# A graph kernel's adjacency build: where TensorE transposes a group of blocks, and when the group is copied out

## The reference

```python
edge_index = jnp.stack([src, dst])
h = jnp.maximum(_layernorm(x), 0.0)
x = x + _L0_gnn_ref(h, edge_weight, src, dst, ...)       # weighted mean over neighbours, both ways, GRU
h = jnp.maximum(_layernorm(x), 0.0)
x = x + _L1_gnn_ref(h, src, dst, edge_weight, alpha)     # 3 hops: segment_sum(w * X[col], row)
h = jnp.maximum(_layernorm(x), 0.0)
x = x + _L2_gnn_ref(h, edge_index, ...)                  # 4 orders: segment_sum(x[row], col) / deg, and attention
h = jnp.maximum(_layernorm(x), 0.0)
x = x + _L3_gnn_ref(h, edge_index, edge_weight1, ...)    # a message per edge, summed by destination
```

## Time and profile before

| | |
|---|---|
| median of 3 runs | 4118.98 us (4118.73 to 4122.45) |
| the profiled execution | 4140.43 us |
| its span in the trace | 4138.6 us |
| busy in the span: PE / DVE / ACT / POOL | 86% / 35% / 31% / 21% |
| build stage, from the first tile to the start of the last window | 50 to 1107 us |
| tiles built; spans; groups copied | 1132; 250; 175 |

### The profile page before, as it was taken

How to read it: one execution, slowest core, us unless ns; L and a number is a source line. 1 busy time by engine, 2 the same in 40 slices (tenths; PEclk the granted TensorE clock), 3 DMA queues, 4 the chain that set the end, 5 groups by cost and what they waited for, 6 DMA issues and landing times. The chain is left out here.

```text
span 4138.6 us, 86265 instructions
## 1 busy us (share of the span) xinstructions
PE 3573.1 (86%) x24482; PEld 2462.8 (60%) x24483; DVE 1462.7 (35%) x4278; ACT 1265.7 (31%) x4012; POOL 873.6 (21%) x929
## 2 busy tenths in 40 slices
PE   5888889999989889968999999997878877877777
PEld 2345556777744444435999999984444545554455
DVE  6766667777602200024321111232222222222223
ACT  5566667788701200014322211232000000000001
POOL 2000000000010000000000000124666666665554
PEclk8999999999999999987999999997988889988889
DMA  2011222323494689851432222341222222222222
GB/s 60 1 46 62 72 67 92 107 94 123 137 233 116 146 197 240 195 139 32 130 107 77 77 77 75 90 114 46 66 64 62 62 62 62 65 63 58 56 59 58
DMA packets 120057, 381.81 MB, mean 92 GB/s; under 512 B 33166, under 2 KB 74620, under 8 KB 106026
## 3 DMA queue, kind: packets, MB, share of 16 engines
q1 hardware_dynamic: 90958, 324.81, 28.9%
q0 software_dynamic: 25664, 51.90, 5.2%
q10 hardware_dynamic: 3154, 1.60, 0.2%
HBM read 294.59 MB, written 83.62 MB: 91 GB/s over the span
## 5 line engine op out<-in xcount | busy, mean ns | idle before, releaser
L2269 POOL DMA_INDIRECT edge_rows<-src_table,src_idx x784 | 778.7, 993 | 482.3 <-issue 187.1
L685 ACT ACTIVATE build_scaled<-build_lanes,w 128x128 f32<-128x128 bf16 x1132 | 428.7, 405 | 307.0 <-DVE build_lanes L640 273.3
L756 PE MATMUL build_ps<-build_keys,build_scaled 128*128 128x300 bf16 (+1 forms) x2264 | 492.0, 299 | 20.6 <-ACT build_scaled L685 17.9
L640 DVE TENSOR_SCALAR build_lanes<-key_id,lane,one_w 128x128 f32<-128x128 f16 x1132 | 388.3, 343 | 237.7 <-PE build_ps L756 182.2
L2416 ACT ACTIVATE edge_act<-edge_ps 128x512 f32<-128x512 f32 x196 | 117.0, 597 | 1160.3 <-remote 742.3
L1108 PE MATMUL prop_ps<-prop_rows,y 125*128 125x500 f32 (+1 forms) x1050 | 408.3, 546 | 44.0 <-DMA prop_rows<-adj_rows 37.0
L748 PE MATMUL build_ps<-build_keys,build_lanes 128*128 128x300 bf16 (+1 forms) x1132 | 345.2, 305 | 87.2 <-DVE build_keys L642 69.5
L2365 PE MATMUL edge_ps<-m_store,edge_hot_t 125*128 x2640 | 234.9, 236 | 207.5 <-issue 133.4
L642 DVE TENSOR_SCALAR build_keys<-key_id,key,win_base 128x300 bf16<-128x300 f16 (+1 forms) x1132 | 404.8, 358 | 0.5 <-issue 0.2
L2350 PE MATMUL edge_ps<-edge_still 128*128 128x512 bf16 x980 | 327.1, 430 | 29.0 <-issue 28.2
L1108 PEld LDWEIGHTS prop_ps<-prop_rows,y 125*128 125x128 f32 x1050 | 188.0, 192 | 263.1 <-issue 195.8
(11 more groups left out here) (371 smaller groups left out, 5029.4 us busy)
## 6 DMA issues: line engine op xcount, KB each, us to landing
prop_rows<-adj_rows SPq DMA_DIRECT2D x85, 1367.2 KB
cnt_panels<-build_cnt SPq DMA_DIRECT2D x50, 683.6 KB
adj_rows<-build_adj_t SPq DMA_DIRECT2D x25, 1367.2 KB
n<-cnt_panels SPq DMA_DIRECT2D x40, 683.6 KB
orders_panel<-cnt_panels SPq DMA_DIRECT2D x40, 683.6 KB
edge_dst_row<-dst_rows SPq DMA_DIRECT2D x196, 125.0 KB
h<-cnt_panels SPq DMA_DIRECT2D x20, 683.6 KB
prop_rows<-adj_rows SPq DMA_DIRECT2D x85, 158.7 KB
```

Of the source, the lines that this page charges most:

```text
L640: v.tensor_scalar(lanes[s][:], g.key_id[:, 0:128], g.lane[:, at], g.one_w3[:, at], ALU.is_equal, ALU.mult).then_inc(s_lanes[s], 1)
L685: a.activation(scaled[s][:], half(lanes[s], 1), ACT.Copy, scale=g.w12[:, bass.ds(t, 1)]).then_inc(s_scaled[s], 1)
L756: last = pe.matmul(ps[:, weight_bank(j), 0:KW[j % 2]], half(scaled[s], i), keys[s][:, 0:KW[j % 2]], start=False, stop=False, skip_group_ch ...
L2269: pool.indirect_dma_start(rows[s][:, i, :], None, dr.table, bass.IndirectOffsetOnAxis(ap=g.src_idx[:, t:t + 1], axis=0)).then_inc(s_rows[s ...
```

## The change

PE no longer transposes a group between the first tile and the pairs of a span, but behind the pairs, ahead of `neighbours` (`turn` moves from `after_first` to `after_last`). DVE and ACT copy a group out one span later than before: group `j - 2` behind span `j`, where it was group `j - 1`. The split of the groups, the one bank, the semaphores and their values, and the code after the last block are as they were.

```diff
--- before.py
+++ after.py
@@ -656,8 +656,8 @@
                     e = d * (WPB // 2) + j // 2
                     spans.tiles(d, j, parity, one(j % 2, e))
                     if parity is not None:
-                        if 1 <= j <= NG and j - 1 in MOVES[0]:
-                            move(v, v.tensor_copy, d - 1, 1 - parity, pair, 0, j - 1)
+                        if 2 <= j <= NG + 1 and j - 2 in MOVES[0]:
+                            move(v, v.tensor_copy, d - 1, 1 - parity, pair, 0, j - 2)
                         if j == SUM_AT[0]:
                             v.wait_ge(s_weight, (d - 1) * WPB + WPB)
                         if j in SUM_AT:
@@ -722,8 +722,8 @@
                     if j >= 2 or parity is not None:
                         low(w - 2, *before(d, j, parity, 2)[:2])
                     if parity is not None:
-                        if 1 <= j <= NG and j - 1 in MOVES[1]:
-                            move(a, copy, d - 1, 1 - parity, pair, 1, j - 1)
+                        if 2 <= j <= NG + 1 and j - 2 in MOVES[1]:
+                            move(a, copy, d - 1, 1 - parity, pair, 1, j - 2)
                         if j == WPB - 1:
                             n1_out(d - 1)
 
@@ -788,7 +788,6 @@
 
             def turn(f, parity, j):
 
-
                 if j == 1:
                     pe.wait_ge(s_weight, f * WPB + WPB)
                 if 1 <= j <= NG:
@@ -807,12 +806,12 @@
                     def after_first():
                         if j >= 2 or parity is not None:
                             rest(w - 2, *before(d, j, parity, 2)[:2])
+
+                    def after_last():
                         if parity is not None:
                             turn(d - 1, 1 - parity, j)
-
-                    def after_last():
-                        if parity is not None and j:
-                            neighbours(d - 1, 1 - parity, j)
+                            if j:
+                                neighbours(d - 1, 1 - parity, j)
 
                     counts.tiles(d, j, parity, pair, one(j, parity), before_first, after_first, after_last)
```

## The result

The changed kernel takes 4186.31 us (median of 4 runs, 4175.2 to 4198.2) where the kernel before takes 4118.93: a ratio of 1.0139, 95% interval 1.0104 to 1.0174. It is slower by 67 us, which the interval puts between 43 and 72 us. The forecast was 4184, slower. For the profiled execution alone it was 4205, which was 17 us too high: the 21.5 us by which the profiled execution of the kernel before stood over its median did not come again.

The account below looks back on a forecast made before the run. PE, busy 86% of the span, was taken to bound the kernel, alone in late blocks, trading waits with DVE and ACT in dense ones. Terms 64 + 27 - 27 + 4.5 - 4 = 64.5, say 65; 4118.98 + 65 = 4184 us, range 4147 to 4216.

Parts of the forecast that it names:

- The moved wait: Behind a span's last tile, PE's transposes wait for ACT's copy of group j - 2, queued behind its windows.
- Terms A and C: A: 49 spans with several pairs stall 1.31 us for ACT's copy, 64 us. C: transposes fill waits for `scaled`, -27 us.
- Term B: One-pair spans: ACT's copy ends late, costing 0.46 us in 31 even and 0.31 in 40 odd spans, 27 us.
- Term D: Spans 4 and 8: DVE's copy, now ahead of a row sum, delays the next first tile; 4.5 us over sixteen spans.
- Term E: Late blocks, span 9 of every second block: DVE no longer loses its lead at span 7; 8 x 0.5, -4 us.
- The sum: Whole build: 64 + 27 - 27 + 4.5 - 4 = 64.5, say 65 us slower.
- one-pair spans hide the wait: Rival: only dense spans stall, as ACT need only come 0.4 us earlier in one-pair spans; 4157 us, chance 0.12.
- The rival of no change: Rival: stalls exist but are offset by larger savings, or PE's time returns where it next waits for keys; chance 0.04.
- The clock: Rival: 1.3 us stalls lower PE's granted clock in dense blocks, some 100 us on top, 4284 us; chance 0.05.
- rule on rotating banks: Groups sharing one bank: each of 120 would pay the copy itself, 0.60 us, 72 us in place of 91.
- The faster rival: At the pairs' end in spans 2, 3, 5, 6, 7 the bank wait is hidden; -26 us, 4093 us, chance 0.04.

Follow-up runs that it names:

- neighbours first: The changed kernel with `neighbours` put ahead of the transposes behind the pairs: 3866.04 us against 3862.8 for the kernel before, ratio 1.0013.
- copy first: The changed kernel with ACT's copy directly behind its tiles, ahead of taking the windows out: 3844.98 us, ratio 0.996 to the kernel before.
- the split: The changed kernel with DVE copying groups 0, 2, 4, 6 and ACT 1, 3, 5: 3904.6 us against 3860.14 for the kernel before, ratio 1.0099.
- the second time: The changed kernel run again unchanged, beside the kernel before: 3921.91 us against 3860.14, ratio 1.0156.

## Why the prediction was right, step by step

**The moved wait** was right and is shown from both sides: filling it (neighbours first) wins 53 us, making the copy early (copy first) wins 74, giving the group to another queue (the split) removes it in just those spans.

**Terms A and C, dense spans** (those with several pairs). In span 5 of block 4 the transposes start 1.23 us late and `neighbours` follows 0.54 behind: 1.23 + 0.07 = 1.30, forecast 1.31. Over the 49 spans the transposes start 61 us late in sum; with the restart that is 65, forecast 64. The stall for `scaled` after dense spans is gone from spans 2 to 8; summed over blocks 1 to 24 (how much later than 0.13 behind its L752 a first tile's L756 starts), it fell from 36 to 8 us: -28, forecast -27. Spans 2, 3, 5, 6 and 7 with several pairs grew by 0.68 to 0.80 us in the median, which is 1.31 less the 0.51 to 0.60 of the boundary ahead of each.

**Term B, one-pair spans,** 0.45 us in even and 0.29 in odd ones by the median, forecast 0.46 and 0.31. In them the transposes start 20 us late in sum, 25 with the restart, forecast 27. The spans themselves grew by 21 in sum, because eight of them follow a dense span and lose its stall of 0.5 us, which term C had counted.

**Term D** was too big: 4.5 forecast; spans 4 and 8 grew by 1.1 us in sum where they have several pairs, and lost 1.4 of stalls for `scaled`, so D is about 2.5. In span 4 of block 4 DVE ends the next first tile's keys 1.24 us after PE gives way from its pairs, where I had added up 1.4. Dense spans 1 grew by 1.9 in sum, which I had not foreseen.

**Term E** was -4 and is -3.3 in the spans 9 with one pair; spans 0 gave another -2.3. The mechanism is as described: of blocks 12, 14, 16, 18, 20 and 22 all but 16 lost 0.7 to 1.0 us in span 9, the odd ones next to nothing.

**The sum.** 64.5 forecast for the build, 58.1 measured (57.3 the second time). The miss is no one term's: B, D and E each came in about 2 us lower and C 1; A and spans 1 together were 3 higher; one-pair spans 4 and 8 and the last window gave back another 2. The three big terms, A, B and C, were right in mechanism and in size. That the time came out at 4186 and not at 4177 is luck: behind the build I forecast nothing. From 4118.93 + 58 there remain 9 us, inside the interval and, with the second pair of measurements, 4. The time behind the mark, in the profiled executions, goes both ways: 3031.5 us before and 3021.3 after in the first pair, 2747.4 and 2759.8 in the second. And the runs of the changed kernel alone spread over 23 us. I call that remainder open, and scatter the likelier reading.

**The rivals.** That one-pair spans hide the wait is refuted by their 0.30 and 0.45. The rival of no change needed a small B; it was 25. The clock stayed at 1.00 in the dense stretch, so stalls of 1.2 us, one per span, didn't bring it down. The Trainium skill (TensorE: Matmul & The Clock Gate, What's actually happening) has the throttled clock as the default that activity releases; these stalls did not bring that default back, while the 4.1 us gap of the earlier trace rows did.

The sum for A and B was 91 by the rows, and the trace shows about 90. The Trainium skill's rule on rotating banks (Perfetto Trace Analysis, Matmuls) pointed the right way; by it alone the estimate was 72. The dense span's 1.23 us against the copy's 0.59 shows the difference: a queue lies ahead of the copy. The faster rival named its own condition, ACT's copy ending before PE's last tile; the kernel with the copy first comes within 0.16 us of that and is 17 us faster in its build, forecast 26.

## What to carry to other kernels

Moving a step behind other work on one engine moves it against the queues of all engines that answer it: ask, for the new place, what stands in the consumer's queue ahead of its answer, and where the producer will be by then. When producer and consumer share a single buffer, both late is no slack: here the copy has to stand directly behind the tiles, ahead of what can wait. And where an engine is given its input only at the end of a span, its own share of the work has to move a span later too, or it stands there and loses its lead, as DVE did when only PE's half was changed.

## What the hardware showed that I had not expected

The kernel before took 4119 and 4130 us in two sets of runs and 3863 and 3860 in two others, with the build the same to 0.3 us. The difference is in the last stage. In the first trace its matmuls of L2350 run from 2848 to 4117 us, in the other from 2840 to 3833, at the same 0.38 us each in the median. Stretches of both (columns as in the earlier trace rows), first the slower:

```profile
3000.00:3200.00 200.00, 157.08 (x1005) 95.92 (x1005) 46.53 (x98) 19.10 (x32) 127.23 (x128) 0.90 0.24 63
```

```profile
3000.00:3200.00 200.00, 171.94 (x1286) 111.78 (x1284) 62.04 (x128) 23.30 (x39) 151.80 (x159) 0.99 0.31 79
```

In 200 us POOL issues 128 gathers there against 159, with PE at a granted clock of 0.90 against 0.99. A gather takes 0.944 us in both in the median, so POOL stands longer between them. The three sets of the experiments ran on three chips, two at 3860 and one at 4130 us, so the chip, or something that goes with it, is the likelier cause; it is not shown. Nor do these runs tell which came first, the clock or the gathers. For the reader of a comparison it means that one change must be measured beside its own base: 260 us of difference here are none of the kernel's.
